# First attention of a two-layer macaron block: the output projection in three rounded products, issued after the next tile's values

## What is computed

```python
qkv = x @ Wqkv_w.T + Wqkv_b            # of the layer norm of x
qkv = qkv.reshape(b, l, 3, H, HD).transpose(2, 0, 3, 1, 4)
q, k, v = (qkv[0], qkv[1], qkv[2])
k = k * SCALE
g = jax.nn.sigmoid(gamma_raw)
def step(state, qkv_t):
    q_t, k_t, v_t = qkv_t
    state = gb * state + jnp.einsum('bhi,bhj->bhij', v_t, k_t)
    y_t = jnp.einsum('bhij,bhj->bhi', state, q_t)
    return (state, y_t)
_, y = jax.lax.scan(step, state0, (qT, kT, vT))
return y @ out_w.T + out_b
...
x = x + _L0_attn_ref(_layernorm(x, axis=-1), ...)
```

## Time and profile before

| | us |
|---|---|
| median of 3 runs (2574.7 to 2575.41) | 2574.9 |
| the profiled execution | 2570.97 |
| its span in the profile | 2568.9 |
| TensorE busy | 2442.4 (95%) |
| VectorE busy | 1842.7 (72%) |
| ScalarE busy | 1420.4 (55%) |
| GpSimd busy | 1285.9 (50%) |

### The profile page before, as it was taken

The page is one execution under the profiler, slowest core; times in us unless marked ns, Lnnn a source line. Parts: engine busy times, 40 slices in busy tenths (PEclk is TensorE's granted clock), DMA queues, the critical chain, the costliest instruction groups (busy, mean ns, idle before and its releaser), DMA issues.

```text
span 2568.9 us, 78013 instructions
## 1 busy us (share of the span) xinstructions
PE 2442.4 (95%) x32232; PEld 2131.2 (83%) x32232; DVE 1842.7 (72%) x4308; ACT 1420.4 (55%) x2361; POOL 1285.9 (50%) x1398
## 2 busy tenths in 40 slices
PE   4999999999999989999999999989999999979999
PEld 3888888888888868888888899878888888858998
DVE  8999899577777789999985766545655565646665
ACT  4555555533334335556665888754544444418886
POOL 5878888621112138889996333213434443453331
PEclk9999999999999999999999999999999999979999
DMA  5000000000000010000000000000000000000111
GB/s 188 1 7 1 1 1 1 1 23 22 24 23 24 23 49 1 1 1 1 1 1 1 18 1 1 1 20 18 18 18 16 17 18 17 18 3 26 34 34 42
DMA packets 67566, 45.97 MB, mean 18 GB/s; under 512 B 13184, under 2 KB 66192, under 8 KB 67216
## 3 DMA queue, kind: packets, MB, share of 16 engines
q1 hardware_dynamic: 67216, 41.00, 5.7%
HBM read 15.78 MB, written 8.40 MB: 9 GB/s over the span
## 4 chain that ended last, share of the span: by engine, by line
PE 69%; issue 14%; POOL 11%; DVE 5%; ACT 2%; DMA 0%; SPq 0%; POOLq 0%; DVEq 0%; ACTq 0%
PE ps L46 11%; PE ps L48 11%; PE ps L47 11%; PE ps L1527 5%; PE ps L1525 5%; PE ps L1506 5%; PE ps L1505 5%; PE ps L612 3%; PE ps L264 3%; PE ps L1172 3%; PE ps L1099 2%; POOL a1pry L2081 2%; POOL a1pry L2083 2%; POOL a1l L2069 2%; PE ps L1130 2%
## 5 line engine op out<-in xcount | busy, mean ns | idle before, releaser
L1570 DVE TENSOR_TENSOR gHl<-gHf,gHh 128x512 fp32r<-128x512 f32 x256 | 186.6, 729 | 184.3 <-ACT gHh L1546 184.1
L231 POOL TENSOR_SCALAR ve<-mv 128x4 f32<-128x4 f32 x96 | 22.2, 231 | 584.4 <-DVE mv L221 580.2
L46 PE MATMUL ps<-WGH,XTH 128*128 128x512 f32 (+1 forms) x768 | 299.6, 390 | 7.3 <-ACT fSG L681 4.4
L48 PE MATMUL ps<-WGL,XTH 128*128 128x512 f32 (+1 forms) x768 | 290.2, 378 | 0.0
L47 PE MATMUL ps<-WGH,XTL 128*128 128x512 f32 (+1 forms) x768 | 289.5, 377 | 0.0
L681 ACT ACTIVATE fSG<-ps 128x704 f32<-128x704 f32 x128 | 97.1, 759 | 312.2 <-PE ps L48 312.2
L827 POOL TENSOR_TENSOR fHTL<-fHTF,fHTH 128x768 fp32r<-128x768 f32 x128 | 236.2, 1845 | 62.2 <-ACT fHTF L690 62.2
L1525 PE MATMUL ps<-W2T,gHh 128*128 128x256 f32 x1024 | 255.4, 283 | 0.0
L1527 PE MATMUL ps<-W2T,gHl 128*128 128x256 f32 x1024 | 253.0, 281 | 0.0
L2069 POOL TENSOR_TENSOR a1l<-a1l,a1rc 128x128 f32<-128x128 f32 x128 | 49.7, 409 | 358.4 <-DVE a1rc L2036 358.4
L46 PE MATMUL ps<-WDH,fHTH 128*128 128x256 f32 x768 | 221.8, 289 | 2.8 <-issue 2.8
(11 more groups left out here) (240 smaller groups left out, 7103.4 us busy)
## 6 DMA issues: line engine op xcount, KB each, us to landing
X<-in_x SPq DMA_DIRECT2D x16, 512.0 KB, 8.8
a0vp<-a0vt SPq DMA_DIRECT2D x256, 32.0 KB, 1.9
a1vp<-a1vk SPq DMA_DIRECT2D x256, 32.0 KB, 2.1
out<-X SPq DMA_DIRECT2D x16, 512.0 KB, 2.9
tws<-in_w SPq DMA_DIRECT2D x2, 1024.0 KB, 7.7
WN<-in_wgu SPq DMA_DIRECT2D x3, 384.0 KB, 5.0
a0km<-in_wqkv SPq DMA_DIRECT2D x2, 384.0 KB, 3.3
a1pry<-in_aw SPq DMA_DIRECT2D x1, 768.0 KB, 4.6
```

The source lines that it names most:

```text
L46: e.matmul(o, hh, mh, start=first, stop=False)
L48: return e.matmul(o, hh, ml, start=False, stop=last)
L1570: dve.tensor_tensor(Hl[m % 8][:, :], Hf[m % 4][:, :], Hh[m % 8][:, :].bitcast(F32), ALU.subtract).then_inc(s_hl, 1)
```

## The change

The output weights are held as a high part `a0OH` and low parts `a0OL0`, `a0OL1` in place of `a0WO`, and tile n's attention as `a0YH` (ScalarE) and `a0YL` (VectorE, from PSUM) in place of two `a0YT` buffers, one buffer each. The projection becomes six `mm3` products (`attn0_out`), and stands in iteration `n` behind the value projection of tile `n`, in front of the key transposes. VectorE adds the result to `X` in front of the decays, makes `a0YL` behind them, and then updates the state. The ring's list follows TensorE's new order. In the setup the weights come by two DMAs beside the other attention weights and a third, `Vt[2]`, which SyncE issues once the FFN before has ended; VectorE makes `a0OL0` of it in the first iteration.

```diff
--- before.py
+++ after.py
...
-        a0YT = [sb(lay0, f"a0YT{i}", [P, D]) for i in range(2)]
-        sb(lay0, "gap1", [P, 288])
+        a0YH = sb(lay0, "a0yh", [P, D], R32)
+        a0YL = sb(lay0, "a0yl", [P, D], R32)
+        a0OL0 = sb(lay0, "a0ol0", [P, D], R32)
+        sb(lay0, "gap1", [P, 32])
...
-        a0WO = sb(lay0, "a0wo", [P, 2, D])
+        a0OH = sb(lay0, "a0oh", [P, 2, D], R32)
...
+        a0OL1 = sb(lay0, "a0ol1", [P, D], R32)
...
@@ -871,11 +878,13 @@
             yield from [("p", 0, o) for o in range(4)]
             for n in range(NT + 2):
                 if n < NT:
-                    yield from [("v", n), *[("s", n, q) for q in range(4)]]
+                    yield ("v", n)
+                if n >= 2:
+                    yield ("o", n - 2)
+                if n < NT:
+                    yield from [("s", n, q) for q in range(4)]
                     if n % 8 < 7:
                         yield ("u", n)
-                if n >= 2:
-                    yield ("o", n - 2)
                 i = n // 4 + 1
                 if n < NT and i < NS:
                     yield from {0: [("t", i, 0), ("t", i, 1)], 1: [("p", i, 0), ("p", i, 1)],
...
         def attn0_set_sp(sp):
-            sp.dma_start(a0WO[:, :, :], wo0.rearrange("(k p) n -> p k n", p=P)).then_inc(d_a0, 16)
...
             for k in range(2):
                 sp.dma_start(KM[0][:, k, 0:768], wqkv[128 * k:128 * k + 128, :]).then_inc(d_wqkv, 16)
+                sp.dma_start(KM[0][:, k, 768:1024], wo0[128 * k:128 * k + 128, :]).then_inc(d_wqkv, 16)
...
         def attn0_set_act(act, n):
 
+            if n == 1:
+                act.activation(a0OH[:, :, :], KM[0][:, :, 768:1024], ACT.Copy).then_inc(s_a0h, 1)
...
-        when0 = (10, 11, 12, 13, 14, 15, 16, 17)
+        when0 = (10, 11, 12, 13, 14, 15, 16, 17, 26)
...
+            if n == 8:
+                dve.wait_ge(s_a0h, 3)
+                dve.wait_ge(d_hank, 96)
+                dve.tensor_tensor(a0OL1[:, :], KM[0][:, 1, 768:1024], a0OH[:, 1, :].bitcast(F32),
+                                  ALU.subtract).then_inc(s_a0l, 1)
...
         def attn0_sp(sp):
+            sp.wait_ge(s_dn, NT)
+            sp.dma_start(Vt[2][:, :], wo0[0:128, :]).then_inc(d_wqkv, 16)
...
+        def attn0_out(pe, p):
+            bank = attn0_take(pe, "o", p)
+            pe.wait_ge(s_yl, p + 1)
+            if p == 0:
+                pe.wait_ge(s_a0l, 4)
+            for k, low in enumerate((a0OL0, a0OL1)):
+                ks = slice(128 * k, 128 * k + 128)
+                t = mm3(pe, bank[:, 0:256], a0YH[:, ks], a0YL[:, ks], a0OH[:, k, :], low[:, :], k == 0, k == 1)
+            t.then_inc(s_op, 1)
+
...
         def attn0_front(pe, n):
...
             t.then_inc(s_vp, 1)
+            if n >= 2:
+                attn0_out(pe, n - 2)
             if j == 0:
...
-                    pe.wait_ge(s_ye, m)
+                    pe.wait_ge(s_yl, m)
...
@@ -1158,6 +1189,8 @@
                     if n:
                         attn0_front(pe, n)
                     scores(n)
+                else:
+                    attn0_out(pe, n - 2)
                 if n == 0:
                     pe.wait_ge(s_xd, NT)
                 if 0 <= m < NT:
@@ -1165,13 +1198,6 @@
                     values(m)
                 if n < NT:
                     grow(n)
-                if n >= 2:
-                    bank = attn0_take(pe, "o", n - 2)
-                    pe.wait_ge(s_ye, n - 1)
-                    for k in range(2):
-                        t = pe.matmul(bank[:, 0:256], a0YT[n % 2][:, 128 * k:128 * k + 128], a0WO[:, k, :],
-                                      start=(k == 0), stop=(k == 1))
-                    t.then_inc(s_op, 1)
                 if n < NT and i + 1 < NS:
                     if j == 0:
                         turn_x(i + 1)
@@ -1195,9 +1221,9 @@
                 i, j = n // 4, n % 4
                 if m >= 0:
                     act.wait_ge(s_av, m + 1)
-                    if m > 1:
-                        act.wait_ge(s_op, m - 1)
-                    act.activation(a0YT[m % 2][:, :], PS[6][:, 0:256], ACT.Copy).then_inc(s_ye, 1)
+                    if m:
+                        act.wait_ge(s_op, m)
+                    act.activation(a0YH[:, :], PS[6][:, 0:256], ACT.Copy).then_inc(s_yh, 1)
                 if n < NT and j == 3:
                     norm(act, *chunk(16 + i + 2))
                 if n < NT and i + 1 < NS:
@@ -1269,16 +1295,25 @@
                 i, j = n // 4, n % 4
                 if n < NT:
                     held(n)
-                    decay(n)
-                    state(2 * n)
-                    if n % 8 < 7:
-                        state(2 * n + 1)
                 if n >= 2:
                     p = n - 2
                     dve.wait_ge(s_op, p + 1)
                     if p % 4 == 0:
                         dve.wait_ge(s_xb, p // 4 + 1)
                     dve.tensor_tensor(X[:, p, :], bank0("o", p)[:, 0:256], X[:, p, :], ALU.add).then_inc(s_xd, 1)
+                if n < NT:
+                    decay(n)
+                if n == 0:
+                    dve.wait_ge(d_wqkv, 80)
+                    dve.tensor_tensor(a0OL0[:, :], Vt[2][:, :], a0OH[:, 0, :].bitcast(F32),
+                                      ALU.subtract).then_inc(s_a0l, 1)
+                if 0 < n <= NT:
+                    dve.wait_ge(s_yh, n)
+                    dve.tensor_tensor(a0YL[:, :], PS[6][:, 0:256], a0YH[:, :].bitcast(F32), ALU.subtract).then_inc(s_yl, 1)
+                if n < NT:
+                    state(2 * n)
+                    if n % 8 < 7:
+                        state(2 * n + 1)
                 if n < NT and j == 2:
                     for k in range(8):
                         stats(dve, *chunk(16 + i + 2), k)
...
```

More of the change, by code:

```diff
@@ L126, in macaron @@
         bot = sb(lay0, "a0bo", [P, D])
-        pw = sb(lay0, "a0pw", [16, 256])
+        pws = ExitStack()
+        pw = sb(pws, "a0pw", [16, 256])
+        pws.close()
+        a0OL1 = sb(lay0, "a0ol1", [P, D], R32)
         rev = sb(lay0, "a0rev", [P, P])
@@ L858, in macaron @@
         s_kx, s_kp, s_sc, s_am, s_it = sem("kx"), sem("kp"), sem("sc"), sem("am"), sem("it")
-        s_av, s_up, s_ss, s_ye, s_op = sem("av"), sem("up"), sem("ss"), sem("ye"), sem("op")
+        s_av, s_up, s_ss, s_op = sem("av"), sem("up"), sem("ss"), sem("op")
+        s_yh, s_yl = sem("yh"), sem("yl")
         entered = lambda j: 15 * (j // 16) + j % 16
@@ L930, in attn0_set_act @@
         def attn0_set_act(act, n):
+            if n == 1:
+                act.activation(a0OH[:, :, :], KM[0][:, :, 768:1024], ACT.Copy).then_inc(s_a0h, 1)
             if n < 2:
-                act.wait_ge(d_wqkv, 32)
+                act.wait_ge(d_wqkv, 64)
                 act.activation(a0WH[:, n, :], KM[0][:, n, 0:768], ACT.Copy).then_inc(s_a0h, 1)
@@ L941, in attn0_set_act @@
                                ACT.Copy).then_inc(s_dte, 1)
-        when0 = (10, 11, 12, 13, 14, 15, 16, 17)
+        when0 = (10, 11, 12, 13, 14, 15, 16, 17, 26)
         def attn0_set_dve(dve, n):
             if n < 2:
-                dve.wait_ge(s_a0h, n + 1)
+                dve.wait_ge(s_a0h, 2 * n + 1)
                 dve.tensor_tensor(a0WL[:, n, :], KM[0][:, n, 0:768], a0WH[:, n, :].bitcast(F32),
@@ L951, in attn0_set_dve @@
             if n == 2:
-                dve.wait_ge(d_a0, 80)
+                dve.wait_ge(d_a0, 64)
                 dve.wait_ge(d_par, 16)
@@ L971, in attn0_set_dve @@
                 dve.tensor_copy(pw[:, 128:129], g1[:, 3:4]).then_inc(s_gb, 1)
-            if n > 5:
+            if n == 8:
[3 more added lines that the diff above has]
+                                  ALU.subtract).then_inc(s_a0l, 1)
+            if n in (6, 7):
                 for j in range(0, 4) if n == 6 else range(4, 7):
@@ L981, in attn0_set_pe @@
             pe.wait_ge(d_hank, 96)
-            pe.wait_ge(d_a0, 80)
+            pe.wait_ge(d_a0, 64)
             src = hankel[:, 0:512] if n == 0 else hankel[:, 512:576]
@@ L995, in attn0_ready @@
         def attn0_ready(e):
-            e.wait_ge(s_a0l, 2)
+            e.wait_ge(s_a0l, 3)
             e.wait_ge(s_bm, 3)
@@ L1314, in attn0_end @@
             e.wait_ge(s_op, NT)
-            e.wait_ge(s_ye, NT)
+            e.wait_ge(s_yl, NT)
             e.wait_ge(s_xd, 64 + NT)
```

## The result

The changed kernel takes 2599.5 us (median of 4 runs, 2590.8 to 2605.3), the kernel before 2574.8 us in the same comparison (4 runs, 2574.4 to 2575.4): a ratio of 1.0093, 95% interval 1.0064 to 1.0122. It is slower, as forecast; the time lies 10.6 us over the forecast of 2588.9 and 2.5 us over the end of the range. Measured once more later, it took 2592.3 us against 2571.5, ratio 1.0083 (1.0070 to 1.0097).

A forecast was written before the change was run, and what follows sets the result against it. The attention stage was taken to go at TensorE's pace. Terms 12.3 + 1.0 + 1.0 + 0.6 - 0.9 = 14.0 us took 2570.97 to 2585.0; with 3.9 for the median, 2588.9 us, range 2580 to 2597.

The forecast's parts named there:

- "issue" pauses: TensorE pauses waiting for no engine: new pauses may swallow part of their 6.5 us, taken as 0.9 us gained.
- blocks: Attention stage: each block of four tiles 0.82 us longer, 15 blocks 12.3 us.
- start: Iteration 0: VectorE waits for a 128 KB load issued after the FFN; bounds 0.33 and 2, taken as 0.6 us.
- last tiles: Last four tiles, where VectorE is dense: added low halves cost between 0 and 1.7 us, taken as 1.0.
- end: After the last `values`: copy, low half and hand-over stand alone; bounds 0.4 and 1.5 us, taken as 1.0.
- Third tile to fourth: Fourth tile's scores wait for ScalarE to finish both key banks; this tile 1.04 us longer, the largest term.
- Second to third: Third tile's scores wait for VectorE's second query operation, which ends earlier; 0.03 us gained, not 0.14.
- Fourth to first: Fourth tile to next block's first: no bank binds, low half in time by 0.06 us; 0.14 us gained.
- First to second: Second tile's scores after VectorE's state updates and low halves, unmoved; shorter updates opening a sequence give 0.05 us gained.
- 0.14 us of saving a tile: TensorE's projection: 0.97 us for the old, 0.71 for six new products, 0.12 paid behind `grow`; 0.14 us saved.
- cheap case of the range: Whole kernel near the range's low end: hand-over 0 and half of the issue pauses gone, 2583 us.
- third rival: Clock falls at every pause before a fourth tile's scores, 15 times, adding 40 us: 2629 us; chance 0.04.

The follow-up runs named there:

- experiments 2 and 4: 2: old plain projection at the new place and ring, against the kernel before, 1.0065. 4: changed kernel with ScalarE's second masked key copy shortened, 1.0053 against the kernel before.
- experiment 3: Kernel before with three products and their halves at the projection's old place, in the old ring: 2578.7 us against 2571.5, ratio 1.0029.
- changed kernel +64: Changed kernel with tile 1's scores issued twice, 64 more TensorE instructions: 2594.3 us against 2571.7 for the kernel before, ratio 1.0087.

## Why the prediction was wrong

The sign, the wait and the largest term were right. The time fell out of the range by one term, the "issue" pauses with the slow clock behind them, which I had taken as small and as a gain. That it came only 2.5 us past the range is partly luck: the blocks had been forecast 2.5 us too long.

| term (us of span) | forecast | measured, first profile / again | |
|---|---|---|---|
| blocks | 12.3 | 9.8 | 14 x 0.63 + 1.0 for the first |
| start | 0.6 | 0.9 | in the first distances, see below |
| last tiles | 1.0 | 0.7 | without the tile with a pause |
| end | 1.0 | 0.1 | |
| "issue" pauses and clock | -0.9 | +10.3 / +7.3 | excess 7.8 / 4.5, and 2.5 / 2.8 in one of the last tiles |
| before the first scores | 0 | 1.1 / 0.7 | differs between kernels with equal work there |
| outside the stage | 0 | 3.7 / 0.3 | differs between executions of one kernel |
| sum | 14.0 | 26.8 / 19.9 | spans' difference |

- **Third tile to fourth** (forecast +1.04): +1.00, 7.47 to 8.47 us. Right, with ScalarE as named; experiments 2 and 4 confirm it.
- **Second to third** (-0.03): -0.07. **Fourth to first** (-0.14): -0.14, and no wait there for the low half. Right.
- **First to second** (-0.05): -0.31 where a tile opens a sequence and -0.02 elsewhere, -0.17 in the mean. Mis-sized by 0.12 us; with small parts of the other three this is the 0.19 us by which a block was forecast too long. VectorE in this tile ran in the forecast order, with no idle time but the 0.30 us for ScalarE's high half:

```profile
628.52 0.42 DVE L1312 TENSOR_TENSOR a0yl<-ps,a0yh 128x256 fp32r<-128x256 f32 x1 [0.30 <-ACT a0yh L1226]
628.87 0.21 DVE L1282 TENSOR_TENSOR a0S<-ps,a0bdp 128x64 f32<-128x64 f32 x1
...
629.75 1.29 DVE L280 TENSOR_TENSOR XTL<-ps,XTH 128x512 fp32r<-128x512 f32 x2
```

- **The 0.14 us of saving a tile** stood: 0.14 to 0.16 in experiment 3. The estimate by the Trainium skill, "FP8 and Floating Point Precision" (TensorE Precision Notes), 0.24 us, is too large for what a tile saves; the rows of before gave the right one.
- **"The new pauses may swallow a part of the 6.5 us of 'issue' pauses: bounds 0 and 6.5"** is the step that failed. I allowed no loss there and had no reason for that: the projection between a tile's short matmuls and the next long products was the thing that I was moving, and the pauses stood right in front of it. They grew from 9.2 us to 15.1 and 13.8, and the clock fell with them at two places of either trace. With this one term at its measured size the sum is 14.0 + 0.9 + 10.3 or 7.3, 25.2 and 22.2 us, and the forecast 2600 and 2597 us: the term alone carries it to the end of the range and past it. Of the 10.3 us, 1.3 is the fall of the clock behind ScalarE's wait; without it the forecast is 2599.
- **Last tiles** (1.0, bounds 0 and 1.7): right. The four distances are 3.2 and 3.5 us longer, but 2.5 and 2.8 of that stand in one of them, 7.01 and 7.29 us long where 4.53 and 4.51 are usual in this kernel: an "issue" pause of 1.03 and 1.31 us and the slow clock with it. That leaves 0.7 us, and in the trace of the changed kernel +64, where no pause falls there, the four are 0.7 us longer than before (20.0 against 19.3). TensorE's waits for VectorE there, and the stage's end, which also shows what became of the earlier trace rows:

```profile
940.64 0.36 PE L46 MATMUL ps<-a0oh,a0yh 128*128 128x256 f32 x1 [0.62 <-DVE a0yl L1312]
...
950.55 0.43 PE L1179 MATMUL ps<-a0vt,a0kp 64*32 64x32 f32 x16 [1.31 <-DVE a0kp L1258]
953.38 1.94 PE L270 MATMUL ps<-ident,fXV 128*128 128x128 f32 x8 [2.39 <-POOL fXV L367]
...
959.59 0.36 PE L46 MATMUL ps<-a0oh,a0yh 128*128 128x256 f32 x1 [1.06 <-DVE a0yl L1312]
```

- **The end** (1.0): the last projection does wait 1.06 us, as worked out, but the stage's end as a whole is only 0.1 us longer. I had not counted that tile 61's projection now stands in front of the last scores and no longer behind them. The transposes there ran at the lower clock before and after.
- **The start** (0.6, bounds 0.33 and 2): the first distance is 0.34 us longer (4.35 against 4.01), which is VectorE's subtraction and nothing more: it follows the decays without idle time, so the load cost nothing. The row:

```profile
521.79 0.41 DVE L1308 TENSOR_TENSOR a0ol<-a0vt,a0oh 128x256 fp32r<-128x256 f32 x1
```

  The second distance is 0.6 us longer (7.19 against 6.60), since by the new order it holds tile 0's projection; with the plain products at the new place it is 7.24. This is the projection that the end has lost. The 1.1 and 0.7 us before the first scores can't be put down to the change: that stretch takes 518.9 to 521.1 us in the traces with halves and 518.2 to 520.5 in those without.
- **The cheap case of the range**: by the prediction's own terms, hand-over 0 and half of the issue pauses gone give 2588.9 - 2.5 - 2.4 = 2584 us and not 2583. Nothing hangs on it.
- **The third rival** (4%): the clock does fall in the stage, but at single places (0.98 over the stage) and not in each fourth tile. Of the three falls up to tile 59 in the first trace one stands behind ScalarE's wait, as the rival has it, at a price of 1.34 us and once in 15; the others stand behind "issue" pauses. It was right that pauses were to be watched, and I watched the wrong ones.

## What to carry to other kernels

In a ring of buffers, moving one user past others changes for all that follow which reader they wait for; count that reader's whole turn, not its last operation. An "issue" pause in the list of waits is a cost that an order can raise or remove: a long group set in the middle of a run of short matmuls took away nearly all of it, where the same group at the run's end did not. What that gave went again, in part into dearer products at that place: no kernel here is faster than the one before by more than the 0.2%. And where a forecast prices a change by a saving of 0.14 us a tile, each term left at "nothing, or a gain" needs its loss bounded too.

## What the hardware showed that was not expected

- Pauses of up to 1.7 us in TensorE's stream without any semaphore, 227 of the 229 of at least 0.15 us ending 1.19 to 1.60 us after a 16 KB packet of the instruction queue landed; 8.5 to 21 us of a stage of about 410, 0 to 3.6 us with the short matmuls broken up 96 and 32.
- The granted clock at 0.50 behind single idle times, at about 1.3 us each: 18 times up to tile 59 in the 18 traces, 17 of them with an "issue" pause of 1.03 to 1.69 us and one behind a 1.08 us wait for ScalarE. Other pauses as long were not followed by a fall.
- The cost of a projection depends on its neighbours: the plain one 0.78 us to the next start before 512-column products and 1.06 before narrow ones, three rounded products 0.71 and 0.89.
